# Router scores of a mixture-of-experts block as four float32 products in column strips, with three qkv tiles moved ahead of them

## The chip, the cores and the metric

One core of one Trainium2 chip runs the whole program. The metric is the device time of one execution in microseconds; the median over the runs of a kernel is compared. Below, TensorE is PE in the profile, VectorE is DVE, ScalarE is ACT, GpSimd is POOL and SyncE is SP.

## What is computed

A normalised input of 1024 tokens by 256 goes through a linear attention with a decay per head and, beside it, through a mixture of experts with top-1 routing and a shared expert; both are added to the input:

```python
xn = _layernorm(x)
qkv = xn @ w_qkv                       # 256 x 768
q, k = elu(q) + 1, elu(k) + 1          # 16 heads of 16
running_kv   = decay_scan(k * v, decay)
running_ksum = decay_scan(k, decay)
den = clip(sum_over_head(q * running_ksum), 1e-6)
attn = (q * running_kv / den) @ w_out
logits = xn @ router_w.T               # 8 experts
gate, expert = sigmoid(max(logits)), argmax(logits)
routed = expert_ffn(expert, xn * gate) # silu(g) * u, 256 -> 2*512 -> 256
shared = (silu(xn @ g) * (xn @ u)) @ shared_down
out = x + attn + routed + shared
```

## The kernel before

Tokens stand in eight tiles of 128, in two halves of 512 (`NH` = 2, `TH` = 4); the model width of 256 is two chunks of 128 (`KC` = 2). TensorE transposes the normalised tokens (`transpose_tokens(n)` for half n) into PSUM banks 4 and 5. ScalarE rounds them to float32r (`x_hi`, L464) and VectorE keeps the rest (`x_lo`, L646), so that a product is made of three float32r matmuls: high by high, low by high, high by low. The weights are split in the same way (`wqkv_hi` and `wqkv_lo`, `sgu_hi` and `sgu_lo`).

The qkv projection has twelve tiles, `qkv_tile(t)`: tile group `a = t // 3` holds k, v and q of one chunk of channels for one half of the tokens (groups 0 and 1 the first half, 2 and 3 the second), six matmuls of 512 columns each, PSUM bank `t % 4`. ScalarE makes ReLU and Exp of tiles 3a and 3a + 2 (L507, L509) into the buffers `rz[:, j]` and `ez[:, j]`; before the ReLU it waits until VectorE has read the buffer's last contents:

```python
act.wait_ge(s_qkv, t + 1)
if a >= 1:
    act.wait_ge((s_k, s_q)[j], a)
```

VectorE turns them into k (`ksum`, L744), k times v (`kvsum`, L747) and q (`q_sb`, L754), in the order of a; in the kernel before `choose()` (the logits' maximum and the chosen expert) stands behind q of group 0 and `place()` (the slot of each token, and the number of tiles of each expert, `plan`) behind q of group 1. Both halves of `sgu_lo`, the low part of the shared expert's weights, are made behind q of group 2 (L762).

The router: `router_logits(n)` multiplies both parts of the router's weights `rT` (16 columns) by `xT_hi` and the high part by `xT_lo`, for one half of the tokens, four matmuls of 512 columns. VectorE and ScalarE copy the 16 rows (`lrow`), `transpose_logits` makes eight transposes of 16 x 128, and `choose` adds the two parts. `ranks` multiplies the chosen experts by a triangle and by ones for `place`. When the slots are known, ScalarE scales the tokens by their gates (`scale_tokens`, behind the Exp of tiles 8 and 9) and GpSimd scatters them to the buffer `sorted_rows`; SyncE loads the first sorted tile of it (L355), and TensorE transposes that in the seventh shared tile.

Behind the twelve tiles TensorE runs seven `shared_tile(k)` (gate part u = 0 and up part u = 1, six matmuls each, PSUM banks `gate_bank[k] + u`), each of which ScalarE (Silu, L538) and VectorE (`hidden`, L788) take out; VectorE runs the scans over k (L738) and the products by q (`q_ksum`, L777) in between. After the fifth shared tile `head_sums` (L1017) needs all four products by q: four float32 products with 32 columns of weights each, every one in a strip of 32 output partitions (`STRIP` = 32) of one bank. Then come the experts' loop (L1105, L1119), the last shared tile, the output projection, and the gather of the routed rows.

No scheduler is at work: each engine runs its own list in the order of the source and waits on counting semaphores.

Of the kernel before, what the change touches and what calls it, by code (L numbers as in the profile page):

```python
# [22 lines left out]
STRIP = 32  # L23


def build(nc, x, w_qkv, w_out, decay_param, router_w, w_gate_up, w_down, shared_gate_up, shared_down, out):
# [21 lines left out]
    with ExitStack() as ctx:  # L48
# [100 lines left out]
        lrow = early[0:2 * E, 0:T].rearrange("p (n t) -> p n t", n=NH)  # L149
# [22 lines left out]
        ROUTE = 6  # L172
        logit_ps = ps[:, 7, 0:NT * 2 * E].rearrange("p (i h e) -> p e i h", h=2, e=E)
# [8 lines left out]
        s_decp = sem("s_decp")  # L182
# [18 lines left out]
        s_rlo = sem("s_rlo")  # L201
# [81 lines left out]
        gate_bank = [4, 0, 2, 4, 0, 2, 4, 2]  # L283
# [7 lines left out]
        bank_user = {3: 0, 4: 1, 5: 2, 6: 3}  # L291
# [81 lines left out]
        def _(pool):  # L373
# [82 lines left out]
        def _(act):  # L456
# [24 lines left out]
            A(rT[:, :, 0, :], ps[:, 7, 0:KC * E].rearrange("p (c e) -> p c e", e=E), ACT.Copy).then_inc(s_rhi, 1)  # L481
# [20 lines left out]
            for a in range(2 * NH):  # L502
                for j, t in ((0, 3 * a), (1, 3 * a + 2)):
# [3 lines left out]
                    A(rz[:, j, :], ps[:, t % 4, :], ACT.Relu, scale=-1.0).then_inc(s_relu, 1)  # L507
                    act.wait_ge(s_relu, 2 * a + j + 1)
                    A(ez[:, j, :], rz[:, j, :], ACT.Exp, scale=-1.0).then_inc(s_er, 1)  # L509
                    if t == 2:  # L510
                        act.wait_ge(s_wlk, 1)
                        act.wait_ge(s_wlv, 1)
                        act.wait_ge(s_wlq, 1)
                        act.wait_ge(s_lrow, NH)
                        A(lrow[:, 1, :], ps[0:2 * E, ROUTE, :], ACT.Copy).then_inc(s_lcopy, 1)
                    if t in (2, 5):
                        c = t // 3
                        act.wait_ge(s_sgu, 16)
                        A(sgu_hi[:, c, :], sgu[:, c, :], ACT.Copy).then_inc(s_shi, 1)
# [665 lines left out]
```

## Time and profile before

| | us |
|---|---|
| median of 3 runs | 129.44 |
| lowest, highest | 129.26, 131.13 |
| the profiled execution | 129.56 |
| its span, first to last instruction | 127.9 |
| around the span | 1.66 |
| TensorE busy, of the span | 122.5 |
| VectorE | 79.7 |
| ScalarE | 52.4 |
| GpSimd | 35.2 |

The profile is of one execution. Its timeline gives each instruction, or a run of the same ones, with its start from the span's start, its duration, and in brackets the idle time before it and what ended that. Matmuls overlap, so the cost of a group on TensorE is the distance from its start to the start of the next group, not its duration.

### The profile page before, as it was taken

The page shows a single profiled execution, that of the slowest core. Times are in us where ns is not written, and L with a number is a line of the kernel's source. Part 1 is how long each engine was busy: PE and PEld are TensorE (multiplying, and loading weights), DVE is VectorE, ACT ScalarE, POOL GpSimd, SP SyncE. Part 2 cuts the span into 40 slices and gives each one's busy share as a digit, 9 for nine tenths or more (in the row PEclk, how much of TensorE's full clock was granted, in tenths as well). Part 3 has the DMA queues.
Part 4 walks back from the last instruction along what each step waited for, and adds up shares of the span by engine and source line. Part 5 has one row for each costly group of instructions (what it writes and reads, how often), then busy time and mean ns, then how long its engine had stood idle before and what let it go on. Part 6 is the DMA issues. An engine that isn't in the chain of part 4 may idle for free.

```text
span 127.9 us, 2432 instructions
## 1 busy us (share of the span) xinstructions
PE 122.5 (96%) x826; PEld 106.6 (83%) x826; DVE 79.7 (62%) x176; ACT 52.4 (41%) x111; POOL 35.2 (28%) x63
## 2 busy tenths in 40 slices
PE   4989999999999999999999999999999999999990
PEld 1258767787888667999999999999999978999990
DVE  0899886999999977755575553515140428922371
ACT  1665796979954725422222222242121337200000
POOL 6804000007888200030303030303030301687500
PEclk9999999999999999999999999999999999999999
DMA  3681999999992210129888988889782031033427
GB/s 95 204 275 60 308 356 243 173 255 399 394 350 109 82 51 0 46 60 293 286 284 290 272 318 264 319 255 336 255 310 75 1 94 51 17 92 96 117 97 243
DMA packets 15748, 25.02 MB, mean 196 GB/s; under 512 B 1296, under 2 KB 12632, under 8 KB 15736
## 3 DMA queue, kind: packets, MB, share of 16 engines
q1 hardware_dynamic: 13368, 20.66, 51.2%
q0 software_dynamic: 1456, 3.41, 8.0%
q10 hardware_dynamic: 912, 0.80, 1.9%
q8 instruction: 7, 0.11, 0.4%
q14 instruction: 5, 0.04, 0.1%
HBM read 18.78 MB, written 6.08 MB: 194 GB/s over the span
## 4 chain that ended last, share of the span: by engine, by line
PE 80%; POOL 6%; issue 5%; DMA 4%; DVE 2%; ACT 0%; DVEq 0%; POOLq 0%
PE ps L1105 25%; PE ps L1119 13%; POOL q_sb L450 6%; PE ps L295 5%; PE ps L296 5%; PE ps L297 5%; PE ps L965 5%; PE ps L971 4%; PE ps L978 4%; PE ps L1049 4%; DMA q_sb<-sorted_rows,slot_row 2%; PE ps L1036 2%; DMA sorted_rows<-yrow 2%; PE ps L1043 2%; DVE x_sb L889 1%
## 5 line engine op out<-in xcount | busy, mean ns | idle before, releaser
L1105 PE MATMUL ps<-xgT,gu 128*128 128x144 f32 x256 | 34.0, 286 | 0.0
L1105 PEld LDWEIGHTS ps<-xgT,gu 128*128 128x128 f32 x256 | 32.3, 190 | 0.3 <-ACT xgT L528 0.2
L820 DVE TENSOR_TENSOR wqkv<-rz,ps 128x288 f32<-128x288 f32 x16 | 7.3, 454 | 25.9 <-ACT rz L564 25.8
L432 POOL DMA_DIRECT2D sorted_rows<-yrow x9 | 5.0, 560 | 55.5 <-DVE yrow L815 55.5
L1119 PE MATMUL ps<-wqkv,dn 128*128 128x144 f32 x128 | 17.4, 289 | 0.0
L564 ACT ACTIVATE rz<-ps 128x288 f32<-128x288 f32 x16 | 6.6, 411 | 25.4 <-PE ps L1105 25.4
L424 POOL DMA_INDIRECT sorted_rows<-xn,slot_row x8 | 11.2, 1396 | 19.0 <-ACT xn L500 17.2
L1119 PEld LDWEIGHTS ps<-wqkv,dn 128*128 128x128 f32 x128 | 16.1, 190 | 0.0
L295 PE MATMUL ps<-xT_hi,sgu_hi 128*128 128x512 f32 x32 | 13.0, 405 | 0.0
L296 PE MATMUL ps<-xT_lo,sgu_hi 128*128 128x512 f32 x32 | 12.5, 390 | 0.0
L297 PE MATMUL ps<-xT_hi,sgu_lo 128*128 128x512 f32 x32 | 12.5, 390 | 0.0
L450 POOL DMA_INDIRECT q_sb<-sorted_rows,slot_row x8 | 8.7, 1083 | 4.5 <-POOLq L446 2.4
L295 PE MATMUL ps<-wqkv_hi,hT_hi 128*128 128x256 f32 x32 | 9.0, 283 | 0.0
L296 PE MATMUL ps<-wqkv_lo,hT_hi 128*128 128x256 f32 x32 | 9.0, 283 | 0.0
L297 PE MATMUL ps<-wqkv_hi,hT_lo 128*128 128x256 f32 x32 | 9.0, 281 | 0.0
L965 PE MATMUL ps<-xT_hi,wqkv_hi 128*128 128x512 f32 x24 | 8.2, 419 | 0.3 <-ACT xT_hi L467 0.3
L567 ACT ACTIVATE yT<-ps 128x256 f32<-128x256 f32 x8 | 3.1, 384 | 12.4 <-PE ps L1119 12.4
L884 DVE TENSOR_TENSOR x_sb<-x_sb,q_sb 128x256 f32<-128x256 f32 x8 | 3.4, 425 | 7.3 <-DMA q_sb<-sorted_rows,slot_row 7.3
L971 PE MATMUL ps<-xT_lo,wqkv_hi 128*128 128x512 f32 x24 | 7.6, 396 | 0.0
L978 PE MATMUL ps<-xT_hi,wqkv_lo 128*128 128x512 f32 x24 | 7.6, 396 | 0.0
L295 PEld LDWEIGHTS ps<-xT_hi,sgu_hi 128*128 128x128 f32 x32 | 6.1, 190 | 1.6 <-issue 0.5
L1049 PE MATMUL ps<-ones 128*128 128x512 bf16 x14 | 5.6, 509 | 1.8 <-POOL ones L377 1.8
(162 smaller groups left out, 230.3 us busy)
## 6 DMA issues: line engine op xcount, KB each, us to landing
gu<-in_L_ffn_w_gate_up_dram SPq DMA_DIRECT2D x8, 1024.0 KB
dn<-in_L_ffn_w_down_dram SPq DMA_DIRECT2D x8, 512.0 KB
sorted_rows<-zeros SPq DMA_DIRECT2D x1, 2592.0 KB, 17.8
wqkv<-sorted_rows SPq DMA_DIRECT2D x10, 144.0 KB
sorted_rows<-yrow POOLq DMA_DIRECT2D x9, 128.0 KB, 2.1
sgu<-_ffn_shared_gate_up_dram SPq DMA_DIRECT2D x1, 1024.0 KB, 6.1
wqkv<-in_L_attn_w_qkv_dram SPq DMA_DIRECT2D x3, 256.0 KB, 3.7
x_sb<-in_L_attn_x_dram SPq DMA_DIRECT2D x2, 256.0 KB, 3.7
```

The source lines that it names most:

```text
L295: nc.tensor.matmul(o, w_hi, m_hi, start=start, stop=False)
L296: nc.tensor.matmul(o, w_hi, m_lo, start=False, stop=False)
L297: return nc.tensor.matmul(o, w_lo, m_hi, start=False, stop=stop)
L424: pool.indirect_dma_start(sorted_rows, bass.IndirectOffsetOnAxis(ap=slot_row[:, i:i + 1], axis=0), xn[:, i, :], None).then_inc(s_scatter, 16)
L450: pool.indirect_dma_start(y_tok[:, i, :], None, sorted_rows, bass.IndirectOffsetOnAxis(ap=slot_row[:, i:i + 1], axis=0)).then_inc(s_gather ...
L820: V.tensor_tensor(hr[:, 2 * h:2 * h + 2, :].rearrange("p f s -> p (f s)"), act_sb[:, h, 0:2 * SLOTS], ps[:, 2 * h + 1, 0:2 * SLOTS], ALU.m ...
L965: mm(o, wqkv_hi[:, kc, cols], xT_hi[:, kc, rows], start=(kc == 0), stop=False)
L971: ins = mm(o, wqkv_hi[:, kc, cols], xT_lo[:, kc, rows], start=False, stop=last and kc == KC - 1)
L978: ins = mm(o, wqkv_lo[:, kc, cols], xT_hi[:, kc, rows], start=False, stop=last and kc == KC - 1)
L1049: mm(ps[:, 0, :], ones[:, :], ones[:, :].unsqueeze(1).broadcast_to([P, 4, P]), start=True, stop=True)
L1105: ins = mm(ps[:, 2 * h + u, (f % 2) * SLOTS:(f % 2 + 1) * SLOTS], gu[p][:, kc, col:col + P], xgT[:, kc, :], start=(kc == 0), stop=(kc == K ...
L1119: ins = mm(ps[:, 5 + c, 0:SLOTS], dn[p][:, f, c * P:(c + 1) * P], hr[:, f, :], start=(f == 0), stop=(f == FC - 1))
```

## The change

- The router's weights `rT` are kept in float32, not split, in a tile of 32 columns per chunk of which the first 8 are used (GpSimd clears it first).
- A float32 copy of the transposed tokens, `xT_raw`, is made: the first half by ScalarE from PSUM (two copies, behind its rounding of the weights), the second half's chunk 0 by GpSimd as the sum of its high and low parts, chunk 1 by VectorE from PSUM, behind `x_lo(1)`.
- `router_logits` is four float32 products, one for each half and chunk, in four strips of 32 partitions of PSUM bank 4. One copy by ScalarE, four transposes of 128 x 128, and the sum over chunks in `choose`.
- TensorE's order: tiles 0 to 3, token transposes of the second half, tiles 4 and 5, router, tile 6, logit transposes, tiles 7 to 11. The decay products and the ranks stand inside tile 8, behind its first two matmuls. The qkv and shared tiles use PSUM banks by a new list.
- ScalarE copies the first half of `sgu_hi` in front of `lrow`. VectorE makes the first half of `sgu_lo` in front of `choose` and the second behind q of group 2; it copies the decay at the start of `place`, and `place` stands in front of q of group 1.

```diff
+        xT_raw = sb("xT_raw", [P, KC, T], F32)
...
-        rT = sb("rT", [P, KC, 2, E], F32R)
+        rT = sb("rT", [P, KC, STRIP], F32)
...
-        lrow = early[0:2 * E, 0:T].rearrange("p (n t) -> p n t", n=NH)
+        lrow = early[:, 0:512]
...
-        ROUTE = 6
-        logit_ps = ps[:, 7, 0:NT * 2 * E].rearrange("p (i h e) -> p e i h", h=2, e=E)
+        LROW = 4
+        ROUTE = 5
+        qkv_bank = [0, 1, 2, 3, 7, 6, 0, 1, 2, 3, 4, 7]
+        logit_ps = ps[:, ROUTE, :].rearrange("p (i c e) -> p e i c", c=KC, e=STRIP)[:, 0:E]
...
-        gate_bank = [4, 0, 2, 4, 0, 2, 4, 2]
+        gate_bank = [0, 2, 4, 0, 2, 0, 4, 2]
...
-        bank_user = {3: 0, 4: 1, 5: 2, 6: 3}
+        bank_user = {3: 0, 4: 1, 5: 3, 6: 2}
...
+            pool.memset(rT[:, :, :], 0.0).then_inc(s_rclear, 1)
...
+            pool.wait_ge(s_xlo, KC + 1)
+            pool.tensor_tensor(xT_raw[:, 0, 512:], xT_hi[:, 0, 512:].bitcast(F32), xT_lo[:, 0, 512:].bitcast(F32), ALU.add).then_inc(s_xraw_pool, 1)
...
-            A(rT[:, :, 0, :], ps[:, 7, 0:KC * E].rearrange("p (c e) -> p c e", e=E), ACT.Copy).then_inc(s_rhi, 1)
+            act.wait_ge(s_rclear, 1)
+            A(rT[:, :, 0:E], ps[:, 7, 0:KC * E].rearrange("p (c e) -> p c e", e=E), ACT.Copy).then_inc(s_rhi, 1)
...
             A(wqkv_hi[:, :, 0:D], wqkv[:, :, 0:D], ACT.Copy).then_inc(s_whq, 1)
+            for c in range(KC):
+                act.wait_ge(s_xlo, c + 1)
+                A(xT_raw[:, c, 0:512], ps[:, 4 + c, :], ACT.Copy).then_inc(s_xraw_act, 1)
...
-                    A(rz[:, j, :], ps[:, t % 4, :], ACT.Relu, scale=-1.0).then_inc(s_relu, 1)
+                    A(rz[:, j, :], ps[:, qkv_bank[t], :], ACT.Relu, scale=-1.0).then_inc(s_relu, 1)
                     act.wait_ge(s_relu, 2 * a + j + 1)
                     A(ez[:, j, :], rz[:, j, :], ACT.Exp, scale=-1.0).then_inc(s_er, 1)
+                    if t in (2, 5):
+                        c = t // 3
+                        act.wait_ge(s_sgu, 16)
+                        A(sgu_hi[:, c, :], sgu[:, c, :], ACT.Copy).then_inc(s_shi, 1)
...
-                        act.wait_ge(s_lrow, NH)
-                        A(lrow[:, 1, :], ps[0:2 * E, ROUTE, :], ACT.Copy).then_inc(s_lcopy, 1)
-                    if t in (2, 5):
-                        c = t // 3
-                        act.wait_ge(s_sgu, 16)
-                        A(sgu_hi[:, c, :], sgu[:, c, :], ACT.Copy).then_inc(s_shi, 1)
+                        act.wait_ge(s_lrow, 1)
+                        A(lrow, ps[:, LROW, :], ACT.Copy).then_inc(s_lcopy, 1)
...
                 dve.wait_ge(s_rank, 1)
+                V.tensor_copy(decay[:, :], ps[:, ROUTE, 256:256 + KC]).then_inc(s_decay, 1)
                 up = mark(V.tensor_tensor_scan(upto[:, :, :].rearrange(flat), restart[:, :, :].rearrange(flat), count_ps, 0.0, ALU.mult, ALU.add))
...
             x_lo(0)
-            dve.wait_ge(s_rhi, 1)
-            V.tensor_tensor(rT[:, :, 1, :], ps[:, 7, 0:KC * E].rearrange("p (c e) -> p c e", e=E),
-                            rT[:, :, 0, :].bitcast(F32), ALU.subtract).then_inc(s_rlo, 1)
...
-            dve.wait_ge(s_wlk, 1)
-            dve.wait_ge(s_wlv, 1)
-            dve.wait_ge(s_wlq, 1)
-            dve.wait_ge(s_lrow, 1)
-            V.tensor_copy(lrow[:, 0, :], ps[0:2 * E, ROUTE, :]).then_inc(s_lcopy, 1)
             x_lo(1)
+            V.tensor_copy(xT_raw[:, 1, 512:], ps[:, 5, :]).then_inc(s_xraw_dve, 1)
...
+            def weight_lo(h):
+                dve.wait_ge(s_shi, h + 1)
+                V.tensor_tensor(sgu_lo[:, h, :], sgu[:, h, :], sgu_hi[:, h, :].bitcast(F32), ALU.subtract).then_inc(s_slo, 1)
+
...
+                V.tensor_tensor(kvsum[:, c, cols], ksum[:, c, cols], ps[:, qkv_bank[3 * a + 1], :], ALU.mult).then_inc(s_kv, 1)
                 if a == 2 * NH - 1:
...
-                if a == 0:
-                    dve.wait_ge(s_decp, 1)
-                    V.tensor_copy(decay[:, :], ps[:, 7, 256:256 + KC]).then_inc(s_decay, 1)
-                dve.wait_ge(s_er, 2 * a + 2)
-                V.scalar_tensor_tensor(q_sb[:, c, cols], ps[:, (3 * a + 2) % 4, :], 1.0, ez[:, 1, :], ALU.add, ALU.max).then_inc(s_q, 1)
-                if a == 0:
-                    choose()
                 if a == 1:
                     place()
+                dve.wait_ge(s_er, 2 * a + 2)
+                V.scalar_tensor_tensor(q_sb[:, c, cols], ps[:, qkv_bank[3 * a + 2], :], 1.0, ez[:, 1, :], ALU.add, ALU.max).then_inc(s_q, 1)
+                if a == 0:
+                    weight_lo(0)
+                    choose()
                 if a == KC:
-                    for h in range(KC):
-                        dve.wait_ge(s_shi, h + 1)
-                        V.tensor_tensor(sgu_lo[:, h, :], sgu[:, h, :], sgu_hi[:, h, :].bitcast(F32), ALU.subtract).then_inc(s_slo, 1)
+                    weight_lo(1)
...
             def transpose_tokens(n):
                 if n:
-                    pe.wait_ge(s_xlo, 2)
+                    pe.wait_ge(s_xraw_act, KC)
...
-            def router_logits(n):
-
-                pe.wait_ge(s_rlo, 1)
-                if n:
-                    pe.wait_ge(s_lcopy, 1)
-                cols = slice(n * 512, (n + 1) * 512)
-                both = ps[0:2 * E, ROUTE, :]
-                pe.wait_ge(s_xhi, 2 * n + 2)
+            def router_logits():
+
+                pe.wait_ge(s_rhi, 1)
+                pe.wait_ge(s_xraw_pool, 1)
+                pe.wait_ge(s_xraw_dve, 1)
+                for g in range(NH * KC):
+                    n, c = g // KC, g % KC
+                    ins = mm(ps[g * STRIP:(g + 1) * STRIP, LROW, :], rT[:, c, :], xT_raw[:, c, n * 512:(n + 1) * 512], start=True, stop=True)
+                ins.then_inc(s_lrow, 1)
+
+            def transpose_logits():
+
+                pe.wait_ge(s_lcopy, 1)
+                out_of = ps[:, ROUTE, :].rearrange("p (n j r) -> p j n r", n=NH, j=TH)
+                for j in range(TH):
+                    ins = tr(out_of[:, j], lrow[:, j * P:(j + 1) * P], ident[:, :])
+                ins.then_inc(s_logit, 1)
+
+            def ranks():
+
+                pe.wait_ge(s_dech, 1)
+                pe.wait_ge(s_chosen, 1)
                 for c in range(KC):
-                    mm(both, rT[:, c, :, :].rearrange("p h e -> p (h e)"), xT_hi[:, c, cols], start=(c == 0), stop=False, skip_group_check=True)
-                for c in range(KC):
-                    pe.wait_ge(s_xlo, 2 * n + c + 1)
-                    ins = mm(both[0:E, :], rT[:, c, 0, :], xT_lo[:, c, cols], start=False, stop=(c == KC - 1), skip_group_check=True)
-                ins.then_inc(s_lrow, 1)
-
-            def transpose_logits():
-
-                pe.wait_ge(s_lcopy, NH)
-                pe.wait_ge(s_decay, 1)
-                for i in range(NT):
-                    n, j = i // TH, i % TH
-                    ins = tr(ps[:, 7, i * 2 * E:(i + 1) * 2 * E], lrow[:, n, j * P:(j + 1) * P], ident[0:2 * E, 0:2 * E])
-                ins.then_inc(s_logit, 1)
-
-            def ranks():
-
-                pe.wait_ge(s_chosen, 1)
+                    mm(ps[:, ROUTE, 256 + c:257 + c], spread[:, c, :], dec_h[:, :], start=True, stop=True)
                 pick = chosen[:, :, :].rearrange("p e i -> p (e i)")
                 mm(rank_ps, before[:, :], pick, start=True, stop=True)
                 mm(count_ps, ones[:, :], pick, start=True, stop=True).then_inc(s_rank, 1)
@@ -952,12 +955,17 @@
                     pe.wait_ge((s_whv, s_whq)[t - 1], 1)
                 if t:
                     pe.wait_ge(s_xlo, 2 * n + 2)
-                if t >= 4:
-                    u = t - 4
-                    pe.wait_ge((s_k, s_kv, s_q)[u % 3], u // 3 + 1)
...
+                if t == 4:
+                    pe.wait_ge(s_rhi, 1)
+                elif 6 <= t < 10:
+                    pe.wait_ge((s_k, s_kv, s_q, s_k)[t - 6], t // 9 + 1)
+                elif t == 10:
+                    pe.wait_ge(s_lcopy, 1)
+                elif t == 11:
+                    pe.wait_ge(s_kv, 2)
...
-                o = ps[:, t % 4, :]
+                o = ps[:, qkv_bank[t], :]
...
                 hi_hi()
+                if t == 8:
+                    ranks()
...
             def shared_tile(k, u):
                 n, f = k // FC, k % FC
+                if k == 0:
+                    pe.wait_ge((s_k, s_kv)[u], 3)
                 if k == 1:
                     pe.wait_ge((s_q, s_k)[u], (3, 4)[u])
-                if k == 2:
-                    pe.wait_ge((s_kv, s_q)[u], 4)
+                if k == 2 and u == 0:
+                    pe.wait_ge(s_kv, 4)
...
             transpose_tokens(0)
-            for t in range(3):
+            for t in range(4):
                 qkv_tile(t)
-            router_logits(0)
             transpose_tokens(1)
-            qkv_tile(3)
-            router_logits(1)
-            pe.wait_ge(s_dech, 1)
-            pe.wait_ge(s_rlo, 1)
-            for c in range(KC):
-                ins = mm(ps[:, 7, 256 + c:257 + c], spread[:, c, :], dec_h[:, :], start=True, stop=True)
-            ins.then_inc(s_decp, 1)
-
             qkv_tile(4)
+            qkv_tile(5)
+            router_logits()
+            qkv_tile(6)
             transpose_logits()
-            qkv_tile(5)
-            qkv_tile(6)
-            ranks()
             for t in range(7, 12):
                 qkv_tile(t)
```

## Rows read from the trace of the kernel before

**Rows 1.** The page: TensorE's busy line (section 1) and its costliest group (section 5).
```profile
PE 122.5 (96%) x826; PEld 106.6 (83%) x826; DVE 79.7 (62%) x176; ACT 52.4 (41%) x111; POOL 35.2 (28%) x63
...
L1105 PE MATMUL ps<-xgT,gu 128*128 128x144 f32 x256 | 34.0, 286 | 0.0
```

**Rows 2.** Timeline (start us, busy us, engine, line), TensorE matmuls, 13 to 32 us.
```profile
13.49 0.62 PE L923 MATMUL ps<-xT_hi,rT 128*16 128x512 f32 x2
...
14.41 1.03 PE L911 MATMUL ps<-ident,xn 128*128 128x128 f32 x8
...
15.20 0.71 PE L965 MATMUL ps<-xT_hi,wqkv_hi 128*128 128x512 f32 x2
...
17.70 0.60 PE L1065 MATMUL ps<-dec_h,spread 16*128 16x1 f32 x4
...
18.23 0.73 PE L965 MATMUL ps<-xT_hi,wqkv_hi 128*128 128x512 f32 x2
...
19.84 0.67 PE L935 MATMUL ps<-ident,wqkv 16*128 16x16 f32 x8
...
20.43 0.74 PE L965 MATMUL ps<-xT_hi,wqkv_hi 128*128 128x512 f32 x2
...
23.43 0.71 PE L965 MATMUL ps<-xT_hi,wqkv_hi 128*128 128x512 f32 x2
...
30.53 0.39 PE L295 MATMUL ps<-xT_hi,sgu_hi 128*128 128x512 f32 x1
...
31.21 0.39 PE L295 MATMUL ps<-xT_hi,sgu_hi 128*128 128x512 f32 x1
```

**Rows 3.** Timeline, the head sums: weight load, products, and the transpose behind them.
```profile
44.34 0.16 PEld L1017 LDWEIGHTS ps<-ksum,head_of 128*32 128x32 f32 x8 [0.35 <-DVE ksum L777]
...
44.35 1.06 PE L1017 MATMUL ps<-ksum,head_of 128*32 128x512 f32 x8
...
45.34 0.33 PE L1020 MATMUL ps<-ident,head_of 128*128 128x128 f32 x1
```

**Rows 4.** Timeline, ScalarE, 11 to 36 us.
```profile
11.99 0.30 ACT L489 ACTIVATE sd<-mv,eps 128x4 f32<-128x4 f32 x1 [1.08 <-DVE mv L624]
...
15.05 1.09 ACT L467 ACTIVATE xT_hi<-ps 128x512 fp32r<-128x512 f32 x2 [0.75 <-PE ps L911]
...
18.82 1.04 ACT L519 ACTIVATE sgu_hi<-sgu 128x1024 fp32r<-128x1024 f32 x1
...
26.51 0.60 ACT L507 ACTIVATE rz<-ps 128x512 f32<-128x512 f32 x1 [0.91 <-PE ps L978]
...
34.58 1.09 ACT L538 ACTIVATE wqkv<-ps 128x512 f32<-128x512 f32 x2
```

**Rows 5.** Timeline, VectorE, 20 to 44 us.
```profile
20.54 0.29 DVE L662 TENSOR_REDUCE logits<-ps 128x64 f32<-128x128 f32 x1 [1.07 <-PE ps L935]
...
22.01 0.22 DVE L669 TENSOR_TENSOR chosen<-em,first 128x64 bf16<-128x64 f32 x1
...
23.54 0.68 DVE L754 SCALAR_TENSOR_TENSOR q_sb<-ps,ez 128x512 f32<-128x512 f32 x1
...
24.14 0.28 DVE L674 TENSOR_TENSOR_SCAN upto<-restart,ps 128x64 f32<-128x64 f32 x1
...
26.46 0.67 DVE L744 SCALAR_TENSOR_TENSOR ksum<-ps,ez 128x512 f32<-128x512 f32 x1
...
28.45 2.35 DVE L762 TENSOR_TENSOR sgu_lo<-sgu,sgu_hi 128x1024 fp32r<-128x1024 f32 x2
...
35.38 0.69 DVE L788 TENSOR_TENSOR sgu<-wqkv,ps 128x512 f32<-128x512 f32 x1 [0.26 <-ACT wqkv L538]
...
42.98 1.28 DVE L777 TENSOR_TENSOR ksum<-q_sb,ksum 128x512 f32<-128x512 f32 x2
```

**Rows 6.** Timeline, GpSimd: the subtraction that splits the q weights.
```profile
10.99 1.30 POOL L417 TENSOR_TENSOR wqkv_lo<-wqkv,wqkv_hi 128x512 fp32r<-128x512 f32 x1 [4.86 <-ACT wqkv_hi L487]
```

**Rows 7.** Timeline, SyncE: the load of the first sorted tile.
```profile
43.93 0.37 SPq L355 DMA_DIRECT2D wqkv<-sorted_rows  x1
```

More of the change, by code:

```diff
@@ L181, in build @@
         s_dec = sem("s_dec")
-        s_decp = sem("s_decp")
         s_wk = sem("s_wk")
@@ L200, in build @@
         s_rhi = sem("s_rhi")
-        s_rlo = sem("s_rlo")
+        s_rclear = sem("s_rclear")
+        s_xraw_act = sem("s_xraw_act")
+        s_xraw_pool = sem("s_xraw_pool")
+        s_xraw_dve = sem("s_xraw_dve")
         s_xhi = sem("s_xhi")
@@ L743, in _ @@
                 dve.wait_ge(s_er, 2 * a + 1)
-                V.scalar_tensor_tensor(ksum[:, c, cols], ps[:, (3 * a) % 4, :], 1.0, ez[:, 0, :], ALU.add, ALU.max).then_inc(s_k, 1)
+                V.scalar_tensor_tensor(ksum[:, c, cols], ps[:, qkv_bank[3 * a], :], 1.0, ez[:, 0, :], ALU.add, ALU.max).then_inc(s_k, 1)
                 dve.wait_ge(s_qkv, 3 * a + 2)
                 dve.wait_ge(s_k, a + 1)
-                V.tensor_tensor(kvsum[:, c, cols], ksum[:, c, cols], ps[:, (3 * a + 1) % 4, :], ALU.mult).then_inc(s_kv, 1)
+                V.tensor_tensor(kvsum[:, c, cols], ksum[:, c, cols], ps[:, qkv_bank[3 * a + 1], :], ALU.mult).then_inc(s_kv, 1)
                 if a == 2 * NH - 1:
                     k_scan(0)
-                if a == 0:
-                    dve.wait_ge(s_decp, 1)
-                    V.tensor_copy(decay[:, :], ps[:, 7, 256:256 + KC]).then_inc(s_decay, 1)
-                dve.wait_ge(s_er, 2 * a + 2)
-                V.scalar_tensor_tensor(q_sb[:, c, cols], ps[:, (3 * a + 2) % 4, :], 1.0, ez[:, 1, :], ALU.add, ALU.max).then_inc(s_q, 1)
-                if a == 0:
-                    choose()
                 if a == 1:
                     place()
+                dve.wait_ge(s_er, 2 * a + 2)
[3 more added lines that the diff above has]
+                    choose()
                 if a == KC:
-                    for h in range(KC):
-                        dve.wait_ge(s_shi, h + 1)
-                        V.tensor_tensor(sgu_lo[:, h, :], sgu[:, h, :], sgu_hi[:, h, :].bitcast(F32), ALU.subtract).then_inc(s_slo, 1)
+                    weight_lo(1)
             k_scan(1)
@@ L1055, in _ @@
             transpose_tokens(0)
-            for t in range(3):
+            for t in range(4):
                 qkv_tile(t)
-            router_logits(0)
             transpose_tokens(1)
-            qkv_tile(3)
-            router_logits(1)
-            pe.wait_ge(s_dech, 1)
-            pe.wait_ge(s_rlo, 1)
-            for c in range(KC):
-                ins = mm(ps[:, 7, 256 + c:257 + c], spread[:, c, :], dec_h[:, :], start=True, stop=True)
-            ins.then_inc(s_decp, 1)
             qkv_tile(4)
+            qkv_tile(5)
+            router_logits()
+            qkv_tile(6)
             transpose_logits()
-            qkv_tile(5)
-            qkv_tile(6)
-            ranks()
             for t in range(7, 12):
```

1 line of the change is left out of this document (added).

## The prediction

> **What bounds the kernel now.** I read four views. The first two lines kept from the page [rows 1] show TensorE at work for 96% of the span, and its costliest group, the experts' float32 products. The timeline of TensorE around the edit [rows 2] shows no gap: each group of matmuls starts where the one before lets go, so every instruction taken out of it is worth its start-to-start distance, if nothing else is then late. Whether something is late is read one stage on. The four head-sum products of L1017 are the only place after the first qkv tile where TensorE's weight load stood until VectorE released it [rows 3]: VectorE's last two products by q end at 42.98 + 1.28 = 44.26 [rows 5], the weight load starts at 44.34, and TensorE's own previous matmul had let go at about 44.26. The two engines arrive there together. So in this kernel TensorE and the pair ScalarE and VectorE are both bounds up to 44.3 us. Behind it TensorE goes on alone without a gap to the experts and the tail.
>
> How far back the second chain reaches: the product at 42.98 is the last of a row of VectorE operations that begins with the first `hidden` at 35.38 [rows 5] and has no gap over 0.22 us (twelve operations: four `hidden`, two scans, two `hidden_lo`, four products by q, 8.88 us in all). That `hidden` waited for the first Silu, which ScalarE started at 34.58 [rows 4]. And ScalarE ran without a gap from 26.51, the ReLU of qkv tile 8, to that Silu: ReLU, Exp, three token tiles scaled, ReLU, Exp, five scaled, ReLU, Exp, table load: 15 instructions, 8.07 us. The ReLU at 26.51 waited for TensorE only.
>
> **TensorE, part by part.** Differences of starts [rows 2]. A plain qkv tile: (30.53 - 23.43)/5 = 1.42, of which the first is some 0.1 dearer because a float32 or bf16 group stands in front of it; I use 1.40 and 0.09 for each such entry. From 13.49 to 30.53 there are 17.04 us, nine tiles are 12.63, the rest 4.41: first router group 0.92 (13.49 to 14.41), transposes of the second half 0.79 (to 15.20), tile 3 and second router group 2.50 (15.20 to 17.70), of which the tile with its entry is 1.49 and the group 1.01, decay 0.53 (to 18.23), eight logit transposes 0.59 (19.84 to 20.43), ranks some 0.07, entries 0.09 to 0.2 each.
>
> After the change: the token transposes cost the same 0.79 + 0.09. The four strip products are the form of L1017, 128x32 weights and 512 float32 columns, four strips, eight records: 44.35 to 45.34 = 0.99 [rows 3], plus the entry 0.08. Bound from above, were they not side by side: an expert record of 144 float32 columns takes 34.0/256 = 0.133 us [rows 1], 512 columns 0.47, the two records of a product 0.94, four products 3.8. From below, nothing makes them cheaper than the same form. I take 0.99, the row is the same instruction. Four wide transposes at 0.79/8 each: 0.40 + 0.09, with 0.05 for their start. Decay and ranks move into tile 8 and cost what they did, 0.53 + 0.07 + 0.08 to re-enter. Sum 3.26 in place of 4.41: TensorE has 1.15 us less to do and would reach the shared tiles at 29.38 instead of 30.53.
>
> **Where TensorE stands now.** Tile 3 13.49 to 14.90; transposes to 15.69; tiles 4 and 5 to 18.58; router to 19.57; tile 6 to 21.05; logit transposes to 21.53, last one landed at 21.75; tile 7 to 23.02; first two matmuls of tile 8 to 23.49; decay and ranks to 24.15; tile 8 to 25.17 (landed 25.37).
>
> **Is the router fed in time?** In the kernel before the first `x_hi` began 0.64 after the transposes began (14.41 to 15.05 [rows 2, 4]), so now at 15.54; with 0.6 for each copy, and 0.69 for a VectorE operation of 512 columns (the one at 35.38 [rows 5]), `x_lo` ends its halves at about 16.87 and 17.47. VectorE's raw copy follows to 18.06. GpSimd's addition has the shape of its own subtraction, 1.30 [rows 6]: 16.95 to 18.25. Both are in front of 18.58, by 0.5 and 0.3. ScalarE's two raw copies, 0.6 each, fill the 1.08 for which it waited for the second variances, to 11.99 [rows 4], so they delay the Sqrt there by 0.1 at most; the extra clearing of `rT` on GpSimd lies in its idle start. Without that cover they would cost 1.1 and some 0.1. On VectorE the raw copy takes the place of the copy of `lrow`, the split of `rT` (0.1) goes.
>
> **VectorE and ScalarE around the routing.** ScalarE: ReLU and Exp of tiles 0 and 2 from 16.59; in the kernel before it was 3.77 from `x_hi` at 15.05 to `sgu_hi` at 18.82 [rows 4] with a copy of `lrow` of 0.5 in between, so `sgu_hi` now begins 3.3 after 15.54, at 18.9 with the later second half of `x_hi`, and ends at 19.94, `lrow` is copied to 20.5, in front of 21.05: no stall. VectorE: the k, kv and q of tile group 0 end about 20.0, then `weight_lo(0)` (half of 2.35 [rows 5]) to 21.1, in what would be a wait for the logits (a wait of 1.07 stands there now, in front of 20.54). So `choose` starts with the last transpose, 21.75 against 20.54: 1.21 later, since a whole qkv tile now stands between the products and their transposes, and token transposes plus two tiles stand before the products. Then by the distances of [rows 5]: `choose`, k and kv 3.00 (20.54 to 23.54), decay copy 0.07, `place` 2.32 (24.14 to 26.46). `chosen` ended 1.69 behind the start at 20.54, so now at 23.44, and 0.08 to a weight load, as in [rows 3], makes 23.52 for TensorE's 23.49: 0.03 of wait. `place` ends at 27.14, where it ended at 26.46.
>
> Now the step that I think decides. `place` was behind q of group 1 and stands in front of it. q of group 1 thus moves from 23.54 to 27.14 and ends at 27.82. ScalarE's ReLU of tile 8 has a wait for exactly that (`(s_k, s_q)[j], a` with a = 2, j = 1: `rz[:,1]` and `ez[:,1]` are free only when q of group 1 has read them). In the kernel before this wait was long met and TensorE ended it (26.51). Now TensorE would let it go at 25.37, but q holds it until 27.85: 1.34 later than before. Queued behind it on ScalarE is all of the 8.07 us listed above, with no gap to give the delay back: first Silu 34.58 to 35.92, first `hidden` 35.38 to 36.72 (VectorE would be ready at about 36.45), last product by q 44.26 to 45.60, head sums 44.34 to 45.68.
>
> TensorE meets two waits for this. `sgu_lo` of the second half: q2 at 29.13, `weight_lo(1)` from 29.73 to 30.93, and TensorE wants it at 29.38 + 0.68 = 30.06: 0.96 of wait, to 31.02 (it was needed at 31.21 and ready at 30.80 [rows 2, 5]). Then it is 0.19 ahead of the kernel before and would start the head sums at 44.15: another 1.53 of wait, to 45.68. Sum: -1.15 + 0.96 + 1.53 = +1.34. Nothing behind gives it back: TensorE has no gap there. The scatter, which follows the scaled tokens, shifts by the same 1.34, and the load of the first sorted tile from 43.93 to 45.3 [rows 7]; TensorE reads that tile in the second half of the seventh shared tile, some 4.8 us behind the head sums, so it isn't late. The profiled execution's 129.56 (span 127.9 and 1.66 around it) becomes 130.9; the median of the runs shown lies 0.12 under that execution, so 130.8.
>
> **The rivals.**
> (B) The hold on the ReLU doesn't bind, or its delay finds slack. Then VectorE's own list decides: from `choose` at 21.75 it has no gap to `weight_lo(1)` and reaches `hidden` at about 35.27 against 35.38. TensorE still waits for `sgu_lo` to 31.02, and the gain is 0.1 to 0.2: 129.3, not slower. It decides where the ReLU of tile 8 starts before 26.51, that is, where q of group 1 ends 1.3 sooner than I have it. Against it: the wait is plainly in the code, and 1.3 us is more than half of `place`.
> (C) All of TensorE's 1.15 reaches the end: 128.3. It needs VectorE's list 1.1 us shorter than its durations; for it speaks only that TensorE is busy for 96% [rows 1].
> (D) GpSimd's addition is late. It has 0.3 of slack; if it takes twice its 1.30 the router, `choose` and the hold on the ReLU move by about 1.0: 131.8. In [rows 6] it ran beside VectorE's statistics, which read one SBUF operand. The Trainium skill, GPSIMD Engine Reference, Specifications, says that GpSimd contends with VectorE where that reads two SBUF inputs or runs a two-port mode; by that rule this addition is undisturbed, since VectorE works there on operands of which one is in PSUM. No row shows the disturbed case.
> (E) The strip products don't run side by side in this place: 3.8 for 0.99, and the logits, `choose` and the hold move by 2.8: 133.6. Against it: [rows 3], the same form in this kernel.
>
> **How the numbers follow.** Forecast 0.68, B 0.10, C 0.07, D 0.08, E 0.04, something else 0.03. The point is the forecast, 130.8; its own range is 130.2 to 131.3 (the eleven operations between the logits and the ReLU, some 0.3 either way, and the runs' scatter). To leave out no more than 2 in 10 the range takes in B and D: 129.2 to 131.8. About 2% is what a measurement of this kernel can tell from no change, here 126.9 and 132.0: slower by more holds E and a little of D, 0.05; faster by more holds nearly nothing, 0.01; within is 0.94.
>
> **What would show it.** Router products at about 18.6, 1.0 long: the TensorE sum. First VectorE reduction of the logits at 21.7. The ReLU of tile 8 at 27.8, put down to VectorE's q: the hold; at 25.4 or 26.5, rival B or C. A wait of TensorE in the first shared tile of about 1.0, put down to `sgu_lo`, and one of 1.5 at the head sums. First Silu at 35.9. TensorE waiting before the router for GpSimd would be D. A granted clock under 1.00 behind the waits, or experts whose weights arrive late after the shift, would add to all of it; nothing in the trace has a wait of this length to show it.

## The result

The changed kernel takes 131.14 us (median of 22 runs, 130.67 to 132.62) where the kernel before takes 129.52 (22 runs, 129.26 to 131.47): a ratio of 1.012, 95% interval 1.0095 to 1.0145. The profiled execution took 131.09, its span is 129.5. TensorE has less to do and the kernel is slower. Ratios leave out executions in a slower state of the chip, over 1.5% above the fastest of their kernel (two of e2 even took 205.80 and 248.05 us, and it is open why); medians and ranges have them all.

The first lines of the page of the changed kernel: the busy shares, and the chain that ended last.

```profile
PE 122.4 (95%) x822; PEld 105.9 (82%) x822; DVE 79.6 (61%) x175; ACT 53.6 (41%) x113; POOL 35.3 (27%) x65
...
PE 72%; DVE 10%; POOL 6%; issue 5%; DMA 4%; ACT 0%; DVEq 0%; POOLq 0%
```

The chain's line on the page of the kernel before:

```profile
PE 80%; POOL 6%; issue 5%; DMA 4%; DVE 2%; ACT 0%; DVEq 0%; POOLq 0%
```

TensorE's share of the chain went from 80% to 72%, VectorE's from 2% to 10%. Timeline of TensorE, the rows that answer to [rows 2, 3]:

```profile
14.89 1.03 PE L917 MATMUL ps<-ident,xn 128*128 128x128 f32 x8
...
18.66 1.06 PE L927 MATMUL ps<-xT_raw,rT 128*32 128x512 f32 x8
19.65 0.74 PE L973 MATMUL ps<-xT_hi,wqkv_hi 128*128 128x512 f32 x2
...
21.16 0.60 PE L935 MATMUL ps<-ident,wqkv 128*128 128x128 f32 x4
21.51 0.70 PE L973 MATMUL ps<-xT_hi,wqkv_hi 128*128 128x512 f32 x2
...
29.42 0.39 PE L300 MATMUL ps<-xT_hi,sgu_hi 128*128 128x512 f32 x1
...
31.05 0.50 PE L300 MATMUL ps<-xT_hi,sgu_hi 128*128 128x512 f32 x1 [0.76 <-DVE sgu_lo L749]
...
45.69 1.06 PE L1029 MATMUL ps<-ksum,head_of 128*32 128x512 f32 x8 [0.66 <-DVE ksum L783]
```

The four strip products take 18.66 to 19.65 = 0.99, the four wide transposes 0.35, and the shared tiles begin at 29.42, 1.11 in front of [rows 2]. Then TensorE stands twice: the profile puts down 0.76 us to `sgu_lo` and 0.66 to VectorE's products by q. The head sums begin at 45.69, 1.34 later than in [rows 3]. ScalarE and VectorE, the rows that answer to [rows 4, 5]:

```profile
27.88 0.60 ACT L519 ACTIVATE rz<-ps 128x512 f32<-128x512 f32 x1 [2.41 <-DVE q_sb L763]
...
35.94 1.09 ACT L550 ACTIVATE wqkv<-ps 128x512 f32<-128x512 f32 x2
```
```profile
21.79 0.29 DVE L674 TENSOR_REDUCE logits<-ps 128x64 f32<-128x128 f32 x1 [0.62 <-PE ps L935]
...
24.89 0.28 DVE L687 TENSOR_TENSOR_SCAN upto<-restart,ps 128x64 f32<-128x64 f32 x1
...
27.11 0.67 DVE L763 SCALAR_TENSOR_TENSOR q_sb<-ps,ez 128x512 f32<-128x512 f32 x1
...
29.78 1.22 DVE L749 TENSOR_TENSOR sgu_lo<-sgu,sgu_hi 128x1024 fp32r<-128x1024 f32 x1
...
36.74 0.69 DVE L794 TENSOR_TENSOR sgu<-wqkv,ps 128x512 f32<-128x512 f32 x1 [0.26 <-PE ps L302]
...
44.35 1.29 DVE L783 TENSOR_TENSOR ksum<-q_sb,ksum 128x512 f32<-128x512 f32 x2
```

ScalarE stood for 2.41 us in front of the ReLU of tile 8 (L519), until VectorE's q (L763, 27.11 + 0.67), which now stands behind `place()`. From there to the first Silu ScalarE has no gap, from the first `hidden` (36.74) to the last product by q (44.35 + 1.29) VectorE has none over 0.2.

### The profile page after: what moved, and what is told of

Its sections match the earlier page's. It is cut to its first block, busy times and chain, and to the rows that moved or that the text cites. A ratio compares the mean times of both kernels' runs of the same rounds, so it can differ in the third digit from the quotient of the medians.

```text
span 129.5 us, 2424 instructions
## 1 busy us (share of the span) xinstructions
PE 122.4 (95%) x822; PEld 105.9 (82%) x822; DVE 79.6 (61%) x175; ACT 53.6 (41%) x113; POOL 35.3 (27%) x65
## 4 chain that ended last, share of the span: by engine, by line
PE 72%; DVE 10%; POOL 6%; issue 5%; DMA 4%; ACT 0%; DVEq 0%; POOLq 0%
PE ps L1108 24%; PE ps L1122 12%; POOL q_sb L458 5%; PE ps L300 5%; PE ps L302 5%; PE ps L301 5%; PE ps L1061 4%; PE ps L973 3%; PE ps L979 3%; PE ps L986 3%; DMA q_sb<-sorted_rows,slot_row 2%; PE ps L1048 2%; DMA sorted_rows<-yrow 2%; PE ps L1055 2%; DVE x_sb L895 1%
## 5 line engine op out<-in xcount | busy, mean ns | idle before, releaser
L432 POOL DMA_INDIRECT sorted_rows<-xn,slot_row x8 | 9.8, 1221 | 14.5 <-ACT xn L512 12.9
```

Of the source, the lines that this page charges most:

```text
L432: pool.indirect_dma_start(sorted_rows, bass.IndirectOffsetOnAxis(ap=slot_row[:, i:i + 1], axis=0), xn[:, i, :], None).then_inc(s_scatter, 16)
```

## The experiments

The theory: the later logits, together with `place()` in front of q, hold the ReLU of tile 8, and this delay goes through ScalarE and VectorE to the head sums. TensorE's 1.15 us end as waits. The rival: the loss lies in the router's new products or in TensorE's new order. All ratios are to the kernel before on the same chip. There are 12 runs of each kernel, but 6 of e3 and of e5, 13 of e6 and 10 of e12; the medians in brackets are of the kernel before, beside them.

| kernel | median us (before) | ratio | 95% interval |
|---|---|---|---|
| e1, q first | 130.23 (129.90) | 1.0036 | 1.0012 to 1.0059 |
| e2, own buffers | 130.10 (129.50) | 1.0032 | 0.9992 to 1.0072 |
| e3, TensorE filled | 131.47 (129.90) | 1.0110 | 1.0056 to 1.0165 |
| e4, before, place first | 130.83 (129.90) | 1.0077 | 1.0038 to 1.0116 |
| e5, router twice | 133.45 (129.90) | 1.0257 | 1.0217 to 1.0297 |
| e6, own buffers, sgu_lo on GpSimd | 130.24 (129.50) | 1.0035 | 1.0003 to 1.0066 |
| e7, own buffers, scaling spread | 130.00 (129.50) | 1.0023 | 0.9990 to 1.0055 |
| e8, all three | 129.89 (129.50) | 1.0000 | 0.9966 to 1.0034 |
| e9, e1 with the old layout | 130.44 (129.53) | 1.0058 | 1.0028 to 1.0089 |
| e10, e8 and the sum on ScalarE | 131.28 (129.53) | 1.0095 | 1.0063 to 1.0128 |
| e11, e10 with the old layout | 130.60 (129.53) | 1.0051 | 1.0019 to 1.0084 |
| e12, before, padded | 130.14 (129.53) | 1.0064 | 1.0025 to 1.0104 |

**The hold taken away in two ways: e1 and e2.** e1 has q of group 1 in front of `place()` again:

```diff
-                if a == 1:
-                    place()
                 dve.wait_ge(s_er, 2 * a + 2)
                 V.scalar_tensor_tensor(q_sb[:, c, cols], ...).then_inc(s_q, 1)
+                if a == 1:
+                    place()
```

> The changed kernel with one step back: q of tile group 1 stands in front of place() again, as in the kernel before. Theory (the ReLU of tile 8 is held by q behind place, and everything queued behind it on ScalarE sets the head sums): the ReLU of tile 8 starts at about 25.4 in place of 27.88, but ScalarE then waits for the slots, which come 0.6 later (27.8), so the first Silu moves from 35.94 to about 34.7 and the time falls by about 1.2, to 129.9. Rival (the loss lies in the router's products, their transposes or the moved tiles): no more than 0.2 of change, 131.1.

e2 leaves `place()` where the change put it and lets tile 8 use two places that nobody else uses at that time, those where the last q and the last product k times v will stand; VectorE's q of group 2 reads `ez8`:

```diff
+        rz8 = q_sb[:, 1, 512:]
+        ez8 = kvsum[:, 1, 512:]
...
-                    if a >= 1:
+                    if a >= 1 and t != 8:
                         act.wait_ge((s_k, s_q)[j], a)
+                    rb, eb = (rz8, ez8) if t == 8 else (rz[:, j, :], ez[:, j, :])
```

> The changed kernel, place() still in front of q of group 1, but ReLU and Exp of tile 8 go to buffers of their own, so that nothing holds that ReLU. Theory: it starts at about 25.4; the scaling then waits for the slots at 27.2; VectorE's own list becomes the bound, its first hidden at about 35.4 in place of 36.74, so the time falls by 1.3, to 129.8. Rival (the hold isn't what costs): 131.1.

Both take back some seven tenths of the loss, from 1.012 to 1.0036 and 1.0032 (the interval of e2 just takes in 1). Timeline of ScalarE and VectorE in e1:

```profile
25.69 0.60 ACT L519 ACTIVATE rz<-ps 128x512 f32<-128x512 f32 x1
...
27.94 1.31 ACT L512 ACTIVATE xn<-xn,gate 128x256 f32<-128x256 f32 x3 [0.99 <-DVE slot_row L705]
...
34.85 1.16 ACT L550 ACTIVATE wqkv<-ps 128x512 f32<-128x512 f32 x2
```
```profile
35.65 0.69 DVE L794 TENSOR_TENSOR sgu<-wqkv,ps 128x512 f32<-128x512 f32 x1 [0.26 <-ACT wqkv L550]
```

The ReLU of tile 8 no longer waits; the scaling now waits for the slots for 0.99, as foreseen, and the first Silu starts at 34.85, 1.09 earlier than with the hold. The head sums began at 45.06, though, and VectorE had its products ready at 44.53: here TensorE was late, by its own. So it was in e2: the ReLU of tile 8 began at 25.40, the first `hidden` at 35.04, the products by q were ready at 44.08, and the head sums began at 44.81. The number of e2 came as expected, but not by VectorE's list, which its theory had as the next bound. That TensorE is late is taken up by e9 and e12.

**TensorE's time at two places: e3 and e5.** e3 puts six matmuls of 512 columns, whose result nobody reads, behind the last qkv tile; e5 makes the router's four products twice.

```diff
             for t in range(7, 12):
                 qkv_tile(t)
+            pe.wait_ge(s_q, 2)
+            for r in range(6):
+                mm(ps[:, 6, :], wqkv_hi[:, r % 2, 0:P], xT_hi[:, r % 2, 0:512], start=True, stop=True)
```

> The changed kernel with six more matmuls of 512 columns (one qkv tile's worth, 1.40 us), results unused, on TensorE between the last qkv tile and the first shared tile. Theory (TensorE's saved 1.15 us is spent waiting for sgu_lo and at the head sums): the two waits shrink by 1.4 together and the time stays at 131.1, within 0.2. Rival (TensorE sets the end in this stage, as its 95% of busy time suggests): 132.5.

> The changed kernel with the four strip products of the router made twice, 1.0 us more on TensorE, in front of the logits. Theory: it delays the logits, choose, place, the ReLU of tile 8 and the head sums by the same 1.0: 132.1, while 1.4 us of TensorE behind the last qkv tile cost nothing. Rival (TensorE's slack at its two waits takes it up): 131.1 to 131.3.

Timeline of TensorE, first of e3 and then of e5:

```profile
45.68 1.06 PE L1029 MATMUL ps<-ksum,head_of 128*32 128x512 f32 x8 [0.75 <-DVE ksum L783]
```
```profile
19.07 1.07 PE L927 MATMUL ps<-xT_raw,rT 128*32 128x512 f32 x8
19.95 1.04 PE L930 MATMUL ps<-xT_raw,rT 128*32 128x512 f32 x8
...
46.95 1.07 PE L1032 MATMUL ps<-ksum,head_of 128*32 128x512 f32 x8 [0.87 <-DVE ksum L783]
```

In e3 TensorE no longer waits for `sgu_lo`, and the head sums began at 45.68 with 1.4 us more work in front of them, 0.01 from where they were, and the ratio (1.011) is that of the changed kernel: in that stage TensorE's time is free. In e5 the second set of products starts 0.88 behind the first. The ReLU of tile 8 and the head sums came 1.26 later each, of which 0.41 is a later start of the whole (first products at 19.07 in place of 18.66): the other 0.85 is carried through the chain one to one. The time rose by more: 1.0257/1.012 is 1.35% or 1.75 us over the changed kernel, for 1.0 expected. In the profiled execution the last gather took 4.1 us to land where those of the changed kernel took 2.8, and VectorE waited 2.20 for it in place of 0.86; why it does so there is open.

**The order alone: e4.** The kernel before with `place()` in front of q.

```diff
+                if a == 1:
+                    place()
                 dve.wait_ge(s_er, 2 * a + 2)
                 V.scalar_tensor_tensor(q_sb[:, c, cols], ...).then_inc(s_q, 1)
                 if a == 0:
                     choose()
-                if a == 1:
-                    place()
```

> The kernel before with one step of the change alone: place() in front of q of tile group 1. Theory: the hold is there too, but the logits come at 20.54, so q ends at about 26.6 and the ReLU of tile 8, which TensorE releases at 26.51, is late by 0.1 to 0.2 only: 129.5 to 129.7. The step costs what the changed kernel lost only together with the later logits. Rival (the order alone makes the loss): about 130.7.

It cost 0.77%, far more than 0.1 to 0.2 us. VectorE and ScalarE in e4:

```profile
23.87 0.29 DVE L674 TENSOR_TENSOR_SCAN upto<-restart,ps 128x64 f32<-128x64 f32 x1
24.73 0.17 DVE L677 TENSOR_SCALAR gone<-gexp 128x8 f32<-128x8 f32 x1 [0.57 <-ACT gexp L522]
...
26.71 0.67 DVE L756 SCALAR_TENSOR_TENSOR q_sb<-ps,ez 128x512 f32<-128x512 f32 x1
```
```profile
24.50 0.19 ACT L522 ACTIVATE gexp<-top 128x8 f32<-128x8 f32 x1
...
27.48 0.60 ACT L507 ACTIVATE rz<-ps 128x512 f32<-128x512 f32 x1 [1.63 <-DVE q_sb L756]
```

`place()` came so early that it waited inside for `gexp` (L522), which on ScalarE stands behind the second half of `sgu_hi`: 0.57 us with q of group 1 behind it. The ReLU of tile 8 started at 27.48, 0.97 later than in [rows 4] (0.24 of it is a later start of this execution). So my price for the order alone was wrong: it holds the ReLU even with the early logits, by another wait. Without the 0.57 and the later start the ReLU would stand at 26.67, the 0.1 to 0.2 late that I had expected (an estimate from these rows). The order alone thus costs some two thirds of what the changed kernel lost, though by a wait that the changed kernel doesn't have. In the changed kernel `gexp` ends at 23.81 and `place()` needs it at 25.08.

**The next bounds: e7, e6, e8.** e7 spreads the scaling of the tokens, e6 has both halves of `sgu_lo` made by GpSimd, e8 has both; all have the buffers of e2.

```diff
-                    if t in (8, 9):
-                        scale_tokens({8: range(0, 3), 9: range(3, NT)}[t])
+                    if t in (9, 11):
+                        scale_tokens({9: range(0, 3), 11: range(3, 4)}[t])
...
                 gate_silu(k)
+                if k < 2:
+                    scale_tokens((range(4, 6), range(6, NT))[k])
```
```diff
+            for h in range(KC):
+                pool.wait_ge(s_shi, h + 1)
+                pool.tensor_tensor(sgu_lo[:, h, :], sgu[:, h, :], sgu_hi[:, h, :].bitcast(F32), ALU.subtract).then_inc(s_slo, 1)
             pool.wait_ge(s_zero, 16)
```

> As with the buffers of its own, and the scaling of the tokens is spread: three token tiles behind Exp 9, one behind Exp 11, two each behind the first two Silus; sgu_lo stays with VectorE. Theory: ScalarE is free early (first Silu at about 32.5), but VectorE's list, with the second half of sgu_lo in it, sets its first hidden at about 35.4: 129.8, no gain over the buffers alone. Rival (ScalarE is the bound once the hold is gone): 128.9.

> As with the buffers of its own, and both halves of sgu_lo are made by GpSimd, which stands idle there, in place of VectorE. Theory: VectorE's list is 1.2 us shorter behind the slots and TensorE no longer waits for sgu_lo; then ScalarE's scaling of the tokens, which starts with the slots at 27.2, sets the first Silu (34.05) and hidden (34.85), 1.9 in front of the changed kernel: 129.2. Rival (VectorE's load isn't the second bound): 129.8, as without it.

> All three: own buffers, sgu_lo on GpSimd, scaling spread. Theory: VectorE's first hidden comes at about 34.2 and its last product by q at about 43.1, where TensorE arrives, so that the 1.15 us saved on TensorE reach the end for the first time: 128.5, 0.9 to 1.0 under the kernel before. Rival (another wait, the late scatter or GpSimd's operations beside VectorE's, eats it): 129.2 or more.

The time of e7 came as foreseen (1.0023 beside 1.0032: no gain that can be told), its reason didn't: VectorE had the products by q at 43.76, and TensorE, which still waited 0.65 for `sgu_lo`, began the head sums at 44.49. e6 and e8 missed: 1.0035 for 129.2 us expected, 1.0000 for 128.5. Timeline of e8, VectorE and GpSimd:

```profile
24.71 0.28 DVE L696 TENSOR_TENSOR_SCAN upto<-restart,ps 128x64 f32<-128x64 f32 x1
24.90 1.17 DVE L699 TENSOR_SCALAR gone<-gexp 128x8 f32<-128x8 f32 x1
25.98 0.21 DVE L701 TENSOR_TENSOR over<-upto,steps 128x64 f32<-128x64 f32 x1
```
```profile
23.63 2.40 POOL L431 TENSOR_TENSOR sgu_lo<-sgu,sgu_hi 128x1024 fp32r<-128x1024 f32 x1 [1.45 <-ACT sgu_hi L532]
```

The addition of 1 to 128x8 elements (L699), 0.15 us in the changed kernel, took 1.17 and ended at 26.07; GpSimd's subtraction ended at 26.03. In e6 the same instruction took 1.14 and ended with GpSimd's too. `place()` is 1.0 longer for it, and this is most of what VectorE had been spared. In e8 the first `hidden` came at 35.37 for the 34.2 expected, and the head sums at 44.32, where they are in the kernel before. The scan (0.28), the copy of the decay (0.15) and the products with an operand in PSUM (0.69) beside the same subtraction kept their times.

The kernel before has the same thing, in a place where it costs little. VectorE beside the subtraction of [rows 6], which ends at 12.29:

```profile
11.58 0.38 DVE L624 BATCH_NORM_AGGREGATE mv<-bn 128x2 f32<-128x6 f32 x4
11.99 0.33 DVE L632 TENSOR_SCALAR ve<-mv 128x4 f32<-128x4 f32 x1
```

The second, an addition to 128x4 elements, ends at 12.32. In e6 it took 0.65 and in e8 0.48, and there too it ended 0.03 and 0.02 behind GpSimd's subtraction; where GpSimd does not hold it, it takes 0.17. The statistics in front of it, on SBUF alone as well, are not held: two of L621 take 0.75 beside the subtraction (from 10.79) and without it (from 8.08), the four aggregates 0.38.

**Is it this instruction or its place? e10.** The addition goes to ScalarE:

```diff
+                        act.wait_ge(s_gexp, 1)
+                        A(gone[:, :], gexp[:, :], ACT.Identity, bias=ones8[:, 0:1]).then_inc(s_gexp, 1)
```

> The kernel with own buffers, sgu_lo on GpSimd and the scaling spread, with one VectorE instruction less: 1 + exp(-top), 128x8 elements, is made by ScalarE. On VectorE that instruction took 1.17 us in place of 0.15 and ended with GpSimd's subtraction at 26.03. Theory (only this one stood behind GpSimd, the operations with two SBUF inputs don't): place() is 1.0 shorter, the slots come at about 26.8, VectorE's hidden at 34.4, the head sums at 43.4: 128.9 to 129.1. Rival (the next SBUF operation of place() waits for GpSimd in its stead): place() as long as before and 129.9.

```profile
25.26 1.00 DVE L702 TENSOR_TENSOR over<-upto,steps 128x64 f32<-128x64 f32 x1
26.18 0.21 DVE L703 TENSOR_TENSOR pos<-upto,ps 128x64 f32<-128x64 f32 x1
```
```profile
23.78 2.39 POOL L431 TENSOR_TENSOR sgu_lo<-sgu,sgu_hi 128x1024 fp32r<-128x1024 f32 x1 [1.46 <-ACT sgu_hi L532]
```

The rival was right: the next operation on SBUF alone, `over` with two SBUF inputs, 0.23 us in the changed kernel, took 1.00 and ended at 26.26, behind GpSimd's end at 26.17. The Trainium skill, GPSIMD Engine Reference, Specifications, names two kinds (VectorE in a two-port mode, or with two SBUF inputs) as those with which GpSimd contends. For `over`, with two SBUF inputs, the runs agree and put a number to it: held to the end of GpSimd's instruction. For the additions with one SBUF input no trace shows in which mode VectorE ran.

This execution of e10, which took 132.83, shows something else. Stretches of it, with TensorE's granted clock as the third figure from the end:

```profile
44.00:45.00 1.00, 0.00 (x0) 0.00 (x0) 1.00 (x3) 1.00 (x3) 0.00 (x0) 1.00 0.09 9
45.00:46.00 1.00, 0.48 (x8) 0.16 (x8) 1.00 (x2) 0.22 (x1) 0.00 (x0) 1.00 0.45 138
46.00:47.00 1.00, 1.00 (x10) 0.49 (x3) 0.87 (x3) 0.00 (x0) 0.00 (x0) 0.84 0.00 0
47.00:48.00 1.00, 1.00 (x4) 0.72 (x4) 1.00 (x2) 0.00 (x0) 0.00 (x0) 0.50 0.00 0
```

TensorE had stood from 43.5 to 45.5 for the head sums (1.98 of it put down to VectorE), and a microsecond later the granted clock was 0.50, to about 50 us. Over the whole of this execution it is 0.987, and the two other runs of e10 with that mean took 132.51 and 132.35; four of e11 with 0.985 to 0.987 took 132.19 to 133.45. The fall is a part of why e10's times scatter (130.02 to 132.91), so its ratio tells little; one run of 132.91 had 0.998. That the stand brought the fall about isn't shown: there is no second trace of it.

**The layout: e9, e12, e11.** In the shared tiles, up to the head sums, three matmuls took 0.68 us in the kernel before (30.53 to 31.21 in [rows 2]) and in e4, and 0.70 in the changed kernel and in e1, e2, e3, e5 to e8 and e10, which are made from it. e9 is e1 with `xT_raw` and `rT` allocated last, e12 the kernel before with unused tiles of their sizes in their places:

```diff
         xT_lo = sb("xT_lo", [P, KC, T], F32R)
+        _pad = sb("pad", [P, KC, T], F32)
...
         rT = sb("rT", [P, KC, 2, E], F32R)
+        _pad2 = sb("pad2", [P, KC * (STRIP - 2 * E)], F32)
```

> The kernel with q in front of place() once more, with xT_raw and rT allocated last, so that every other tile has its old place in SBUF. There the shared tiles ran at 0.70 us for three matmuls against 0.68 in the kernel before, and TensorE came to the head sums at 45.06, 0.5 behind the last product by q. Theory (the places of the tiles in SBUF make the difference): 0.68 again, head sums at about 44.6, 129.6 to 129.8. Rival (the order of PSUM banks or of TensorE's list makes it): 0.70 and 130.2 as without.

> The kernel before, with unused SBUF tiles of the sizes that the change adds at the places where it adds them; no instruction differs. Theory (places in SBUF): the shared tiles run at 0.70 for three matmuls, nine half tiles reach the head sums 0.4 later, and the time rises by 0.4 to 0.6, to 129.9 to 130.1. Rival (banks or order): 129.4, unchanged.

> That kernel with xT_raw and rT allocated last as well. Theory (places in SBUF): TensorE reaches the head sums some 0.4 earlier, where VectorE then sets the time, and the three shared halves behind them are 0.04 shorter each: 0.1 to 0.5 under the one without, 128.6 to 128.9, the fastest of all. Rival (places don't matter): the same as without, within 0.1.

Timeline of TensorE, the first matmul of a triple and that of the eighth triple behind it, and the head sums, in e12 and then in e9:

```profile
34.76 0.40 PE L297 MATMUL ps<-xT_hi,sgu_hi 128*128 128x512 f32 x1
...
40.34 0.39 PE L297 MATMUL ps<-xT_hi,sgu_hi 128*128 128x512 f32 x1
...
44.61 1.07 PE L1019 MATMUL ps<-ksum,head_of 128*32 128x512 f32 x8
```
```profile
34.98 0.39 PE L301 MATMUL ps<-xT_hi,sgu_hi 128*128 128x512 f32 x1
...
40.42 0.39 PE L301 MATMUL ps<-xT_hi,sgu_hi 128*128 128x512 f32 x1
...
44.59 1.06 PE L1030 MATMUL ps<-ksum,head_of 128*32 128x512 f32 x8
```

Eight triples take 5.58 us in e12, 0.70 each, and 5.44 in e9, 0.68 each. In e12 no instruction differs from the kernel before, so the places of the tiles in SBUF make the difference; which place matters isn't shown. The place isn't all there is to it either: behind the head sums two triples of the kernel before take 0.69 and 0.70 (46.21 to 47.60). The head sums of e9 began at 44.59, as expected, 0.47 in front of e1's; 0.17 of it was there at the third triple already (32.16 for 32.33), 0.30 is the rate. What it is worth in time is less sure: e12 is 0.64% or 0.83 us slower than the kernel before (interval 0.25 to 1.04%), where 0.4 to 0.6 us were expected, but e9 (1.0058) is not faster than e1 (1.0036), and its runs reach from 129.63 to 131.30. e11 ran at 0.68 and still stood 1.59 us for VectorE at the head sums, so the layout could not show there. e11 was expected at 128.6 to 128.9 and is at 1.0051. In e10 and e11 one `hidden` of VectorE waited 1.28 and 0.56 us for a tile that TensorE's records show as ended before; I have no reason for that.

No version was faster than the kernel before; e8 can't be told from it (interval 0.9966 to 1.0034, its median 0.4 us above).

## Why the prediction was right

**TensorE's sum.** Products 0.99, transposes 0.35 (0.40 expected), decay and ranks as before, shared tiles at 29.42 (29.38 expected), 1.11 gained for 1.15. Right, though the terms as they are listed behind the change add up to 3.17, not 3.26; the places of the next paragraph go with 3.26, and so did the trace.

**The feeding of the router.** GpSimd's addition ran from 16.93 for 1.29 us, VectorE's copy ended at 18.04, the products began at 18.66: 0.08 later than the sum had it, without a wait for either. Rival D did not come, nor E. D says that no row shows a disturbed operation; the trace of the kernel before had one, the addition at 11.99 shown above, 0.16 longer beside the subtraction of [rows 6].

**The logits and `place()`.** 21.79 for 21.75, `place()` to 27.11 for 27.14.

**The hold.** ReLU of tile 8 at 27.88 for 27.85, first Silu at 35.94 for 35.92, head sums at 45.69 for 45.68. e1 and e2 take the hold away and seven tenths of the loss go with it; e3 shows that TensorE's own time is free behind it, e5 that the time in front of the logits is not. This step is shown. e4 adds that the order alone costs more than the step says, by the wait for `gexp`.

**The two waits.** Here one size was off. They were to be 0.96 and 1.53. Counted as the prediction does, by distances of starts, they are 0.93 (30.12 to 31.05) and 0.81 (44.88 to 45.69); the 0.76 and 0.66 of the profile leave out the end of the matmul in front. The second is short because TensorE reached the head sums at about 44.9, not at 44.15. From the restart to there it took 13.83 us for 19 triples, where it took 13.05 in the kernel before. Some 0.35 of the 0.78 between them is the rate of 0.70 for 0.68, since the change also moved tiles in SBUF. Most of the rest lies behind the first wait, where from the second triple to the third (31.05 to 32.20) are 1.15, 0.19 of it idle "issue". Why is open; e3, e6 and e8, which don't wait for `sgu_lo`, have no such gap. The size did not matter for the end, as it hides in front of VectorE; it matters for what is left once the hold is gone, and e1 shows it.

**Rival B** had the ReLU not held and expected 129.3. With the hold really gone e1 and e2 stood at 1.0036 and 1.0032, some 129.9: I had not seen that TensorE would then come last, at the head sums 0.5 and 0.7 behind VectorE's products, after its wait for `sgu_lo`, the slow start behind that and the rate of 0.70; in e1 ScalarE also waits for the slots, for 0.99.

**The end.** 1.34 expected behind the head sums; the gather began 1.49 later than before (111.03 for 109.54) and the span grew by 1.6. The 0.3 between 130.8 and what the ratio gives (129.52 x 1.012 = 131.1) is about what the span of the profiled executions grew behind the head sums (1.6 less 1.34); of that 0.07 lies in the three half shared tiles up to the experts, the rest wasn't followed. It was small enough to leave the forecast right.

## What to carry to other kernels

Time taken from the engine that is busy for 96% of the span was worth nothing here, since a second chain ended beside it: before counting a saving, look at the next place where that engine waits for another, and follow the other's list back to its last gap. When an operation is moved in front of another on one engine, look up who waits for the one that was passed, above all for the release of a buffer; here a wait that had always been met became the one that decides. And adding a tile in the middle of the allocation changes the addresses of all behind it, so a before and after comparison should hold the layout fixed where a few tenths matter.

## What the runs showed of the hardware

- Two kinds of VectorE operations on SBUF alone stood until GpSimd's running subtraction ended: additions of a constant (128x8: 0.15 became 1.17 us in e8; 128x4: 0.17 became 0.33 to 0.65 in the kernel before, e8 and e6) and one with two SBUF inputs (0.23 became 1.00 in e10). The layer norm's statistics on SBUF (0.75 for two, 0.38 for four aggregates, kernel before) and operations with an operand in PSUM (e8) did not.
- The place of tiles in SBUF changed the rate of float32r matmuls of 512 columns from 0.68 to 0.70 us for three, with the same instructions (e12).
- In the profiled execution of e10 TensorE stood for 2.0 us, and about a microsecond after it had taken up work again its granted clock fell to 0.50, that is 1.2 GHz, for some 3 us; in those of e11 and e6, with stands of 1.59 and 1.23 us at the same place, it stayed at 1.00.
